# A fused attention and slot-routing kernel: the first pair's way to its features, set-up products in shared banks

## What is computed

```
x = x + attn(layernorm(x))
x = x + ffn(layernorm(x))

# attn, for one batch row, n = 512 tokens
q     = tanh(x @ W_charge.T + b_charge)                 # one number a token
phi_c = mags * q ** [0, 1, 2, 3, 4]                     # five powers
shell = normalize(x @ W_shell.T + b_shell)              # 64 numbers, divided by their norm
proj  = shell @ omega.T + rff_bias                      # 32 angles
phi_s = [cos(proj), sin(proj)] * scale                  # 64 numbers
phi   = (phi_c x phi_s, flattened: 320) @ W_combine.T   # 64 features
attn  = softmax(causal(phi @ phi.T * T / temp))         # T decays with distance
out   = (attn @ (x @ W_v.T + b_v)) @ W_out.T + b_out

# ffn, for one batch row
h      = gelu(x @ w1a.T + b)           ; logits = h @ w2.T + b2        # 64 slots
alpha  = softmax over the top 8 of the logits
slots  = GRU(alpha.T @ x / sum(alpha), slot_init)
out    = (alpha @ (slots @ wv.T + bv)) @ wo.T + bo
```

## Time and profile before

| what | value |
|---|---|
| median of three runs | 741.21 us |
| profiled execution | 737.18 us |
| its span (first to last instruction) | 735.4 us |
| mean granted TensorE clock | 0.996 |
| PE busy | 713.3 us, 97% |
| PE weight loads | 547.6 us, 74% |
| DVE busy | 589.8 us, 80% |
| ACT busy | 428.4 us, 58% |
| POOL busy | 389.1 us, 53% |
| DMA queue q1 | 53.63 MB, 25.8% of 16 engines |

### The profile page before, as it was taken

The page is one execution under the profiler, slowest core; times in us unless marked ns, Lnnn a source line. Parts: engine busy times, 40 slices in busy tenths (PEclk is TensorE's granted clock), DMA queues, the critical chain, the costliest instruction groups (busy, mean ns, idle before and its releaser), DMA issues.

```text
span 735.4 us, 14788 instructions
## 1 busy us (share of the span) xinstructions
PE 713.3 (97%) x4546; PEld 547.6 (74%) x4546; DVE 589.8 (80%) x1821; ACT 428.4 (58%) x840; POOL 389.1 (53%) x838
## 2 busy tenths in 40 slices
PE   7988999999899999999999999999999999999996
PEld 4966777777696877778687777869777777866774
DVE  4878777777988888897988889797888889786755
ACT  3357485736457574655658566564857565565351
POOL 5626767343655738375564828465573837544300
PEclk9999999999999999999999999999999999999999
DMA  6362211202323041323214032322404132121005
GB/s 209 114 175 56 57 31 28 50 8 75 100 87 86 1 145 30 115 59 115 59 40 129 6 115 59 115 59 67 107 2 134 39 116 58 58 58 59 1 3 171
DMA packets 49429, 55.09 MB, mean 75 GB/s; under 512 B 6022, under 2 KB 40392, under 8 KB 49352
## 3 DMA queue, kind: packets, MB, share of 16 engines
q1 hardware_dynamic: 48578, 53.63, 25.8%
q10 hardware_dynamic: 774, 0.53, 0.3%
HBM read 20.58 MB, written 16.78 MB: 51 GB/s over the span
## 4 chain that ended last, share of the span: by engine, by line
PE 87%; ACT 3%; SPq 2%; DVE 2%; DMA 2%; issue 2%; POOL 1%; DVEq 0%; ACTq 0%; POOLq 0%
PE ps L399 17%; PE ps L288 16%; PE ps L314 15%; PE ps L425 8%; PE ps L474 6%; PE ps L370 5%; PE ps L538 4%; PE ps L349 4%; PE ps L459 4%; PE ps L437 2%; PE ps L518 2%; PE ps L351 2%; SPq L1425 2%; POOL Z L232 1%; PE ps L282 1%
## 5 line engine op out<-in xcount | busy, mean ns | idle before, releaser
L399 PE MATMUL ps<-VS,ET 128*128 128x257 f32 x640 | 159.5, 383 | 0.1
L399 PEld LDWEIGHTS ps<-VS,ET 128*128 128x128 f32 x640 | 112.6, 190 | 23.5 <-issue 11.1
L232 POOL TENSOR_TENSOR Z<-Z,QB 128x512 f32<-128x512 f32 x60 | 76.3, 1272 | 98.8 <-ACT Z L703 97.1
L661 ACT ACTIVATE xn<-X,rs 128x256 f32<-128x256 f32 x128 | 66.2, 593 | 59.2 <-POOL rs L1263 59.2
L722 ACT ACTIVATE ET<-ps 128x128 f32<-128x128 f32 (+3 forms) x128 | 55.1, 431 | 64.8 <-PE ps L288 64.6
L314 PE MATMUL ps<-W1h,xh 128*128 128x354 f32 x256 | 87.5, 342 | 1.3 <-DVE biasM L1076 1.0
L854 DVE TENSOR_TENSOR VS<-ps,biasM 128x354 f32<-128x354 f32 x128 | 66.2, 524 | 28.1 <-PE ps L314 27.8
L712 ACT ACTIVATE E<-ps,nmax 128x128 f32<-128x128 f32 (+3 forms) x128 | 64.4, 529 | 38.5 <-DVE nmax L923 38.2
L314 PE MATMUL ps<-W1l,xh 128*128 128x354 f32 x256 | 83.3, 326 | 0.0
L314 PE MATMUL ps<-W1h,xl 128*128 128x354 f32 x256 | 82.9, 324 | 0.0
L242 POOL TENSOR_SCALAR xm<-X,rs 128x256 f32<-128x256 f32 x120 | 65.4, 560 | 4.6 <-POOL rs L1284 4.6
(11 more groups left out here) (188 smaller groups left out, 1600.1 us busy)
## 6 DMA issues: line engine op xcount, KB each, us to landing
X<-in_x SPq DMA_DIRECT2D x32, 512.0 KB, 4.2
xmT<-Z SPq DMA_DIRECT2D x128, 128.0 KB, 2.3
out_x<-X SPq DMA_DIRECT2D x30, 512.0 KB, 3.3
out_x<-X SPq DMA_DIRECT2D x4, 256.0 KB, 2.3
X<-in_gru_whhT SPq DMA_DIRECT2D x1, 768.0 KB
wih<-in_gru_wihT SPq DMA_DIRECT2D x1, 768.0 KB
X<-in_W_v ACTq DMA_DIRECT2D x1, 256.0 KB, 4.4
X<-in_W_outT ACTq DMA_DIRECT2D x1, 256.0 KB, 5.0
```

The costliest lines, as they stand in the source:

```text
L232: e.tensor_tensor(Z[:, i + 1, :], Z[:, i, :], QB[:, :], ALU.mult).then_inc(s["zm"], 1)
L399: ins = e.matmul(p[:, 0:D + 1], ET[:, r % 2, j * 128:j * 128 + 128], VS[:, (2 * k + d) % 4, j, 0:D + 1], start=j == 0, stop=j == i)
L661: ins = e.activation(xn[:, d, t, :], X[:, b % NX, t, :], ACT.Identity, bias=rs[:, d, 2, t:t + 1], scale=rs[:, d, 1, t:t + 1])
```

## The change

Six things are changed, all in the written-out beginning and end; the loop body of iterations 3 to 14 is as before.
- Loads: SP loads row 1 directly behind row 0, without waiting for the weights. Four small loads are added (wx, parts of W_combine on the partitions opposite to wc's). Rows 4 to 9 are loaded in one batch.
- Norms: for pair 0 the six variance operations are done by DVE (scale_a_setup, scale_b_setup); POOL does the power and the last product. The two column copies bcA and bcS move from POOL to ACT.
- phi(0): no moves. Ten products with 64 rows and 64 columns, two for each of the five powers, each issued when its power is there. wc, wx and w4 are chosen so that every power meets its part of W_combine.
- Set-up products share banks: three banks instead of seven takes; two evacuations instead of three for the bias.
- Order: pair 0's and pair 1's steps, and those of pairs 2 to 4 in the written-out part, stand in another order on every engine. The thirteen warm-up products before q_t(0) are gone.
- End: hidden(z, 0) stands before gx_n(y), behind three warm-ups; small exchanges on ACT and DVE.

```diff
-        SETUP, SOFT, CHAIN, SLOTS = 7, 9, 5, 12
-        POOL_LN, POOL_TEMP, SLOT_POOL = 13, 20, 5
+        SETUP, SOFT, CHAIN, SLOTS = 6, 10, 5, 12
+        POOL_LN, POOL_TEMP, SLOT_POOL = 17, 24, 5
+        def ln_variance_ops(e, k, d):
+            b = 2 * k + d
+            e.wait_ge(s["ln_s"], 4 * b + 4)
...
+            e.tensor_tensor(mv[:, d, :, :], stats[:, d, :, 1:3], stats[:, d, :, 4:6], ALU.add).then_inc(s["ln_a"], 1)
...
+            e.tensor_tensor(rs[:, d, 0, :], rs[:, d, 0, :], rs[:, d, 1, :], ALU.add).then_inc(s["ln_v"], 1)
@@ phi (PE)
+                if k == 0:
+
+                    e.wait_ge(s["soft"], SOFT)
+                    e.wait_ge(s["zc"], 1)
+                    for i in range(5):
+                        if i:
+                            e.wait_ge(s["zm"], i)
+                        for d in range(2):
+                            w = w4[own(d), d, :] if i == 4 else (wc if i % 2 == d else wx)[own(d), i // 2, :]
+                            ins = e.matmul(p[own(d), :], w, Z[own(d), i, :], start=i == 0, stop=i == 4)
+                    ins.then_inc(s["phi"], 1)
+                    return
                 e.wait_ge(s["zm"], 4 * k + 4)
-                e.wait_ge(s["zs"], 128 * (k + 1))
+                e.wait_ge(s["zs"], 128 * k)
@@ weights_setup and bias_setup (PE)
-                    setup(2 * c, [(wv_n[:, z, cs], woT[:, z, :]) for z in range(2)], "setup_mm", "setup_evac")
-                    setup(2 * c + 1, [(wsh[:, cs], omT)], "setup_mm", "setup_evac")
+                    p, _ = G.take(s["setup_evac"], 2 * c + 2)
+                    at["setup_mm", c] = p
+                    columns_of(p, 0, [(wv_n[:, z, cs], woT[:, z, :]) for z in range(2)])
+                    columns_of(p, 322, [(wsh[:, cs], omT)]).then_inc(s["setup_mm"], 1)
@@ order (PE)
-            weights_setup(); xn_t(0, 0, 0); xn_t(0, 0, 1); bias_setup(); proj(0, 0, 0); proj(0, 0, 1)
+            weights_setup(); xn_t(0, 0, 0); xn_t(0, 0, 1); bias_setup(); xn_t(0, 1, 0); proj(0, 0, 0)
@@ end (PE)
-            gx_rz(y); xm_t(z, 0, 0); xm_t(z, 0, 1); gx_n(y); hidden(z, 0); xm_t(z, 1, 0); xm_t(z, 1, 1)
+            gx_rz(y); xm_t(z, 0, 0); xm_t(z, 0, 1)
             e.wait_ge(s["E"], 8 * NP)
             warm(3)
+            hidden(z, 0); xm_t(z, 1, 0); xm_t(z, 1, 1); gx_n(y)
             hidden(z, 1)
@@ scalar
+            def columns():
+                e.wait_ge(s["wb"], 16 * 5)
+                e.activation(bcA, bvc.unsqueeze(2).broadcast_to([128, 2, 128]), ACT.Copy).then_inc(s["columns"], 1)
+                e.activation(bcS, bshc.broadcast_to([64, 128]), ACT.Copy).then_inc(s["columns"], 1)
@@ sync
-                if b == 1:
-
-                    e.wait_ge(s["wa"], 16 * 5)
+                if k == 0:
+                    return
+                for m in range(4):
+                    load(wx[oth(m % 2), m // 2, :], a["W_combineT"][64 * m:64 * m + 64, :], "w")
-            load_x(0); weight_loads(); load_x(1); first_loads(); load_x(2); load_x(3); slot_loads()
-            load_x(4); load_x(5); z_moves(0); load_x(6); load_x(7); load_x(8); z_moves(1); load_x(9)
-            z_moves(2)
+            load_x(0); load_x(1); weight_loads(); load_x(2); first_loads(); load_x(3); slot_loads()
+            load_x(4); load_x(5); load_x(6); load_x(7); load_x(8); load_x(9); z_moves(1); z_moves(2)
```

More of the change, by code:

```diff
@@ L111, in build @@
         w4 = sb("w4", [128, 2, C])
-        wcs = sb("wcs", [128, 3])
+        wx = sb("wx", [128, 2, C])
+        wcs = sb("wcs", [128, 5])
         U = sb("U", [128, N])
@@ new lines, in _ @@
+            proj(3, 1, 2); proj(3, 1, 3); e_t(2, 0); xm_t(1, 0, 1); e_t(2, 1); values(2, 0); logits(2, 1)
+            e_t(2, 2); xm_t(1, 1, 0); e_t(2, 3); values(2, 1); xm_t(1, 1, 1); hidden(1, 0); values(2, 2)
+            q_t(3); hidden(1, 1); xn_t(4, 0, 1); e_t(2, 4); xn_t(4, 1, 0); gather(0); route(1); logits(2, 2)
+            gi_t(0); z_t(3); values(2, 3); values(2, 4); gx_n(0); e_t(2, 5); gx_rz(0); e_t(2, 6)
+            values(2, 5); xn_t(4, 1, 1); rt_t(1); e_t(2, 7); values(2, 6); phi(3); values(2, 7)
@@ L618, in _ @@
+            z_t(4); e_t(3, 5); gx_rz(1); gx_n(1); values(3, 4); e_t(3, 6); values(3, 5); e_t(3, 7)
+            values(3, 6); slot_v(1); values(3, 7); al_t(1); phi(4); gather(2); logits(4, 0); out_mm(1, 0)
+            gi_t(2)
             for it in range(3, NP - 1):
```

307 lines of the change are left out of this document (153 added, 154 removed).

## The result

| kernel | median us | lowest to highest | runs | ratio to before (95%) |
|---|---|---|---|---|
| before, same chip | 741.10 | 738.89 to 742.20 | 4 | |
| changed | 732.04 | 730.03 to 732.47 | 4 | 0.9876 (0.9847 to 0.9905) |

The change makes the kernel 1.2% faster. The profiled execution of the changed kernel took 732.47 us (span 730.6, mean granted clock 0.994), where the prediction's own sum gave 732.2.

The account below looks back on a forecast made before the run. PE was taken to pace the repeated middle but to wait during the first 60 us. A net 4.7 us from the beginning plus 0.3 at the end made 5.0 us less: median 741.21 to 736.2 us, range 732.6 to 740.2.

Parts of the forecast that it names:

- step 6: Pair 0's maxima through phi(1): phi(1) 6.9 us sooner, less 2.2 us of PE work standing behind it, net 4.7 us.
- the order of pairs 1 to 3 also removes waits: Rival for pairs 1 to 3: another 2 us or so gained, 734 us; chance 0.12.
- the half-rate clock as a risk: Within the rival that most is given back (738.7 us, chance 0.19): a second half-rate stretch, 1.7 us each.
- a sign of error: The forecast would be wrong if the granted clock showed half-rate for more than one stretch.
- Step 1: Row 1 loaded right away: removes the stall to 7.13 us; weights land about 1.1 us later, nothing on the path.
- Step 2: Variance operations shared with DVE, 1.3 us a row: first projection at 17.0 instead of 17.94, 0.9 us gained.
- Steps 3 and 4: Slot products start at 26.6 to 27.5; warm-ups gone, projections done by 43, last power ends at 46.7, DVE the bound.
- Step 5: phi(0) without moves: 64-row halves overlap, 0.9 us after the last power; logits near 49.7 instead of 56.22, 6.5 us sooner.
- the rival of the Z chain: Late Z copies on ScalarE make PE wait before phi(1) to phi(3): about 2 us slower, 743.2; chance 0.09.
- Step 7: The end: hidden(z,0) moved ahead, so the last xmT copy before the table load comes about 0.3 us sooner.

Follow-up runs that it names:

- a_tail: The changed kernel with the written-out end of PE, ACT and DVE as before: 731.12 us, ratio to before 0.9886.
- a_fill3: The changed kernel with 2 warm-ups added before the slot setup and 6 before the first exponential's transpose: 730.34 us, ratio to before 0.9881.
- b_fill: The kernel before with 28 more warm-up products in TensorE's waits of the first 57 us: 737.94 us, ratio to before 0.9989.
- a0: The changed kernel, unedited, run again in a later set: 731.18 us, ratio to before 0.9890.
- b_early: The kernel before with row 1 loaded directly behind row 0, without waiting for the weights: 742.55 us, ratio to before 1.0043.
- b_cols: b_early with GpSimd's two column copies moved behind both rows' norm scales: 735.59 us, ratio to before 0.9949.
- a_wait: The changed kernel with row 1 loaded behind the weights and waiting for them again: 737.69 us, ratio to before 0.9955.
- b_two: b_cols plus the 64-row phi(0) without moves, wx loaded behind row 2: 737.05 us, ratio to before 0.9955.
- a_moves: The changed kernel with phi(0) over moved copies again, the moves issued behind the loads of rows 4 to 9: 739.96 us, ratio 1.0005.

## Why the prediction was wrong, step by step

**The step that failed** is the last of the sum: "the median of the runs, 741.21, lies 4.0 above it, and I move it by the same". This gives the median the same 5.0 us as one profiled execution. The medians moved by 9.1 in the first comparison and by about 8.0 over all runs. Before's median lay 4.0 us above its profile, the changed kernel's 0.4 below. Before's profiled 737.18 lies in the fastest tenth of its own 90 further runs, with a mean clock of .996 where these average .992, and the changed kernel's 732.47 is the slowest of its four, at .994.

That the sum's 732.2 for the profiled execution came out as 732.47 is partly luck. **The term that was too small is step 6's,** net 4.7 us: it takes 2.2 us off the 6.9 of phi(1) for PE work behind it. a_tail's profile, the changed kernel with the old end, has one half-rate stretch in its head as before's has (33.4 to 36.8 us there, 18.9 to 22.3 before), so these two are alike in clock. The multiplication by U of pair 5 in before, the changed kernel and a_tail, one line from the timeline of each:

```profile
240.84 0.69 DVE L913 TENSOR_TENSOR QK<-ps,U 128x512 f32<-128x512 f32 x1 [0.38 <-PE ps L351]
...
236.20 0.69 DVE L957 TENSOR_TENSOR QK<-ps,U 128x512 f32<-128x512 f32 x1 [0.39 <-PE ps L387]
...
233.82 0.69 DVE L956 TENSOR_TENSOR QK<-ps,U 128x512 f32<-128x512 f32 x1 [0.38 <-PE ps L387]
```

At like clock the gain there is 7.0 us, not 4.7 (7.5 at pair 1, 7.3 at pair 3), so little of the 2.2 us was lost, and 6.3 reach the end of the profiled execution (737.18 to 730.92). In the changed kernel's own profile a second stretch, near 53 us, had taken 1.4 us of this by pair 3, and a longer wait at phi(4) another 1.0. The rival that came nearest was "the order of pairs 1 to 3 also removes waits", 734, at a chance of 0.12: phi(2)'s wait of 1.07 us is gone.

So the sum gave 5.0, and three things came on top. About 1.5 us more are gained at equal clock (6.3 by the two profiles, 6.6 by the fits). **The sum had no term for how the change alters the clock:** the prediction charged the half-rate clock as a risk of the new order, yet over all runs the changed kernel loses less full clock (2.5 us against 5.9), worth about 1.4 us by the fits; a_fill3 and b_fill point the same way. The profile has two stretches in the head, which the prediction had named as a sign of error, and here it was no such sign. The last 1 us is the first comparison's own: there before ran at 741.1, against 739.4 elsewhere, and the changed kernel at 732.0 against 731.4. Why stays open: the set is small and each set ran on its own chip.

The steps, by the changed kernel's own profile (two half-rate stretches in the head), a_tail's (one) and a0's (none); starts in us:

| step | predicted | changed | a_tail | a0 |
|---|---|---|---|---|
| first projection | 17.0 | 16.6 | 16.7 | 16.6 |
| slot products | 26.6 to 27.5 | 26.5 | 26.6 | 26.5 |
| angles | 34.0 | 34.6 | 34.2 | 34.0 |
| last power (its end) | 46.7 | 47.2 | 47.3 | 45.8 |
| first logits | 49.7 | 50.1 | 50.2 | 48.7 |
| first transpose of an exponential | 52.8 | 52.9 | 53.0 | 51.5 |
| Z(1) copied | 61.5 | 62.2 | 60.9 | 59.3 |
| phi(1) | 69.9 | 70.7 | 69.4 | 67.8 |
| multiplication by U of pair 5 (240.8 before) | 236.1 | 236.2 | 233.8 | 233.8 |

- *Step 1, row 1 early:* the sum holds, its reading does not. "Nothing on the path" is right for the changed kernel's early row only because the variance and the copies have left GpSimd's way. With the old queue the same edit costs 3.3 us, together with one moved line it gains 3.6 (b_early, b_cols), and taken out of the new order it costs about 6.5 (a_wait). The copies' wait for the weights on GpSimd is in the trace of before, and I bounded the later landing by VectorE's use alone.
- *Step 2, norms:* the six operations of a row took 0.96 us together (6.92 to 7.88) against my 1.3, and row 0 is normalised from 9.45 against 9.7. The direction was right; at the projection the step is worth 1.4 us, not 0.9.
- *Steps 3 and 4:* right to 0.6 us. The slot products start on time although POOL is not ready near 25 as I had it, but near 26.4; PE waits 0.60 us for it. DVE is the bound to the last power, as predicted (busy 8.9 of the 9 us from 38 to 47). But PE does not wait with phi(0): the projections end at 44.20 instead of 43, the twenty instructions follow without a gap, and the last four start 0.5 us behind the last power.
- *Step 5:* the halves overlap: two instructions start within 0.01 us of each other (44.20 and 44.21), the next two 0.43 to 0.48 us later, so sixteen take 3.48 us to the last four at 47.68, 0.217 each, as predicted from the earlier trace rows. The TensorEngine Tiling (Array Packing) page of the Trainium skill, Key Properties, says that tiles work independently and that a change of mode drains. The trace agrees with the first; of a drain it shows no more than 0.1 us (0.25 us from the projection's last instruction at 43.95 to 44.20, where 0.16 is usual). But the cause was put wrongly. The step credits phi without moves with the time that the moves took; b_two shows that in the old order this is worth nothing. That the order (projections of pair 1 done while the angles are made) is what makes it pay is the reading that fits b_two and a_moves; how much it pays there was not measured by itself.
- *Step 6:* predicted net 4.7, and 4.6 in the profile (240.8 to 236.2), but 7.0 at like clock, as above. phi(1) to phi(3) wait for nothing, so the rival of the Z chain fell. What I had not looked at is pair 4: PE waits 1.97 us at its phi, 2.48 in a0 and 0.93 in a_tail, for moves that land later than before's (a median of 4.9 to 5.5 us against 3.5). a0 comes to pair 3 8.8 us ahead and to pair 4 only 6.6. That is why a0 without a stretch in its head is no further at pair 5 than a_tail with one. What delays these moves was not tested.
- *Step 7, the end:* 0.3 predicted; the medians show nothing, the profiles 0.4 to 0.6 (a_tail).

The parts do not add up. Measured one at a time in the old order, the early row loses 3.3 us and the 64-row phi 3.6; together with two repairs, of GpSimd's queue and of SP's, they gain 3.2; the whole change gains 8. The remaining 4 to 5 us are everything else: the new order on all engines with the phi that it seems to make pay, the norms on DVE, the shared banks, the batch of loads. The shared banks and the order by itself were not run alone, so how these microseconds divide stays open.

## What to carry to other kernels

A gain read from one profiled execution is that execution's gain. Before it is given to the median, compare its granted clock with that of the other runs, and ask whether the change alters how often the clock falls. When a sum comes out right, look whether the two profiles are alike in clock before calling it right. When a transfer is moved, follow not only who waits for it but who waits for the ones it delays, on every queue: here a half-megabyte row ahead of a few bytes of bias cost 3.3 us, and the same row gained 3.6 once the steps that wait for the bias stood behind the row's norm. And a wait that is removed is only worth what the next instruction in that engine's list can use; with eight projections in front, moves that nobody waits for are free.

## What was not expected of the hardware

- The same program spreads over 6.8 us in 90 runs with a mean granted clock between .985 and .998; a microsecond of full clock lost costs about 0.55 us in before and 0.66 in the changed kernel. A part of it costs nothing: in the profiles of these two kernels the clock is at half again from 1 to 3 us after PE has finished.
- In a wait of 3.44 us the clock fell to half and stayed there for 13.7 us, though PE was busy 4.2 and then 5.0 us of the windows of 5 us that followed (b_early).
- Small VectorE operations (128 by 4 or 8) cost 0.16 to 0.17 us each, and six in a row, most of them waiting for the last, took 0.96 us.
- Eight moves of 128 KB behind six rows of 512 KB took a median of 4.9 us to land, against 2.3 over the changed kernel's whole profile.
